# A selective-scan and attention block on one core: two PSUM banks for the jobs, new spacing, and the window softmax divided behind the values' product

## The reference, cut to what matters

```
h = exp(dt[:, :, None] * A) * h + (dt * xt)[:, :, None] * bt[:, None, :]     # the scan, for each t
y = einsum("bdn,bn->bd", h, ct)
scores = einsum(q of 32 tokens, k of the 96 tokens around) / sqrt(8) + bias, masked
attn   = softmax(scores, axis=-1)
ao     = attn @ v3 ;  attn_out = ao @ wo                     # 16 heads, 4 key/value heads
es     = x @ dec.T / sqrt(128) ; eo = softmax(es) @ dec      # memory lookup
x + 0.2*attn_out + 0.45*ssm_out + 0.15*silu(conv) + 0.2*(x @ w_wm + b + 0.3*eo)
```

## Time and profile before

| what | value |
|---|---|
| median of 3 runs | 1167.07 us (1165.49 to 1168.94) |
| the profiled execution | 1166.9 us, span 1165.1 us |
| busy DVE / POOL / PE / ACT | 988.3 / 951.5 / 866.0 / 835.1 us |
| granted TensorE clock, mean | 0.830 of full |

### The profile page before, as it was taken

One profiled execution on the slowest core, in us unless ns is written; L12 is line 12 of the kernel. 1 busy time (PEld: TensorE's weight loads), 2 busy tenths in 40 slices (PEclk: granted clock), 3 DMA queues, 4 the chain that ended last, 5 costly groups with the idle time before them and its releaser, 6 DMA issues. The chain is left out here.

```text
span 1165.1 us, 19124 instructions
## 1 busy us (share of the span) xinstructions
PE 866.0 (74%) x4151; PEld 361.1 (31%) x4151; DVE 988.3 (85%) x2306; ACT 835.1 (72%) x2247; POOL 951.5 (82%) x668
## 2 busy tenths in 40 slices
PE   4477769687786787777786777867768687778775
PEld 2132323232333233333232333323233233333332
DVE  2699998888897997979989799788998989898992
ACT  4668786877778776777777777587776876766671
POOL 6479997988888887888979898698887988788892
PEclk8558998778897977979889788787989788897797
DMA  5845766565756566566656476555666566656640
GB/s 121 202 127 147 199 164 171 133 169 163 181 153 159 156 158 165 146 155 167 165 166 165 118 192 169 141 147 148 173 167 177 137 166 169 174 157 173 159 113 9
DMA packets 124397, 181.18 MB, mean 156 GB/s; under 512 B 29266, under 2 KB 41062, under 8 KB 124262
## 3 DMA queue, kind: packets, MB, share of 16 engines
q1 hardware_dynamic: 123974, 179.56, 58.9%
q10 hardware_dynamic: 288, 0.20, 0.1%
HBM read 170.79 MB, written 5.05 MB: 151 GB/s over the span
## 5 line engine op out<-in xcount | busy, mean ns | idle before, releaser
L1391 POOL TENSOR_TENSOR prod<-hst,C 128x1024 f32<-128x1024 f32 x256 | 601.7, 2353 | 156.7 <-DVE hst L1201 155.9
L1201 DVE TENSOR_TENSOR_SCAN hst<-decay,bank 128x512 f32<-128x512 f32 x384 | 459.5, 1206 | 16.0 <-POOL prod L1391 15.1
L659 ACT ACTIVATE decay<-wide,A_rep 128x512 f32<-128x512 f32 x384 | 273.9, 715 | 72.8 <-DVE hst L1201 55.0
L1189 DVE TENSOR_TENSOR bank<-bank,B 128x512 f32<-128x512 f32 x384 | 261.7, 681 | 48.8 <-PE bank L938 23.0
L905 PE MATMUL bank<-spread,sel_bc 96*128 96x512 bf16 x384 | 170.0, 444 | 145.3 <-DVE hst L1201 137.0
L673 ACT ACTIVATE prob<-s_sb,nmax 128x96 f32<-128x96 f32 x512 | 184.8, 363 | 1.5 <-DVE nmax L1214 0.5
L1407 POOL TENSOR_TENSOR uwide<-uwide,B 128x512 f32<-128x512 f32 x128 | 162.7, 1271 | 21.8 <-DMA uwide<-u_rows 21.8
L929 PE MATMUL bank<-prod,sel_red 128*32 128x512 f32 x1024 | 171.7, 750 | 2.0 <-POOL prod L1391 2.0
L1201 DVE TENSOR_TENSOR_SCAN hst<-bank,uwide 128x512 f32<-128x512 f32 x128 | 155.0, 1211 | 6.1 <-ACT bank L659 4.6
L938 PE MATMUL bank<-k,q 128*128 128x384 f32 x256 | 133.6, 609 | 7.3 <-DVE nmax L1214 4.8
L945 PE MATMUL bank<-ident,prob 128*96 128x128 f32 x512 | 99.4, 328 | 48.9 <-ACT ao L689 44.2
(11 more groups left out here) (188 smaller groups left out, 1014.6 us busy)
## 6 DMA issues: line engine op xcount, KB each, us to landing
wide<-dt_rows SPq DMA_DIRECT2D x512, 256.0 KB, 4.6
uwide<-u_rows SPq DMA_DIRECT2D x128, 256.0 KB, 4.1
spread<-parts SPq DMA_DIRECT2D x66, 32.0 KB, 3.4
x_sb<-in_L_attn_x_dram SPq DMA_DIRECT2D x8, 256.0 KB, 4.1
dt_rows<-sp_t SPq DMA_DIRECT2D x8, 256.0 KB, 3.9
out_dram<-outb SPq DMA_DIRECT2D x8, 256.0 KB, 2.3
vw<-v_tok SPq DMA_DIRECT2D x80, 16.0 KB, 3.3
u_rows<-uv SPq DMA_DIRECT2D x8, 64.0 KB, 3.6
```

Of the source, the lines that this page charges most:

```text
L659: nc.scalar.activation(to, wide[m % SLOTS][:, s % 2, :], ACT.Exp, scale=A_rep[:, g:g + 1]).then_inc(exp_done, 1)
L1189: v.tensor_tensor(uP[s % 4][:, :], uP[s % 4][:, :], B2[p][:, :], ALU.mult).then_inc(dbx_done, 1)
L1201: v.tensor_tensor_scan(hst[:, s % 4, :], kept, into[:, :], 0.0, ALU.mult, ALU.add).then_inc(scan_done, 1)
L1391: g.tensor_tensor(prod[:, 2 * (m % 4):2 * (m % 4) + 2, :], hst[:, 2 * (m % 2):2 * (m % 2) + 2, :], C2[p][:, :].unsqueeze(1).to_broadcast([ ...
```

## The change

Four things change.

1. **Banks.** Bank 3 becomes `memP` and carries the nine "m" jobs; `jobP` keeps the others. `fill` keeps a predecessor for each of the two. The decay factors of q = 3 no longer lie in bank 3: the tile `decay` has four places in SBUF, and the scan of q = 3 reads `decay` and `uwide`.
2. **Spacing.** All jobs have new slots, the "m" jobs from slot 10 on (28 before), v, q and k of the next batch at 37, 52 and 56 (58, 60 and 62 before). Jobs are emptied one slot later than they are filled (`EMPTY_LAG` 1). Output comes three slots behind the feed-forward product (one before), the convolution's gate two slots behind its tanh (one before). In the last batch the ten first products of the projection stand in slots 48 to 63, where six stood in slots 58 to 63 and four behind the slots.
3. **Softmax.** The probabilities stay undivided. The transposition stands 6 slots behind the scores (9 before), the values' product 8 (11 before). Behind it PE multiplies the inverted sums, spread over 32 columns, by the identity, into columns 128 to 255 of the same bank; ACT copies both halves to `ao_raw`, and POOL multiplies them into `ao4` (`output_norm`, 9 slots behind the scores). `prob_norm` is gone.
4. **Value windows.** SP waits for the first scores of the batch, too, before it issues them.

```diff
-JOB_AT = {13: ("t", "back"), 15: ("p", "xaT"), 17: ("p", "xnT"), 19: ("p", "dtpre"),
-          22: ("t", "zT"), 26: ("t", "ffn"), 28: ("m", "es0"), 32: ("p", "B"), 33: ("p", "C"), 34: ("m", "pt0"),
...
+JOB_AT = {14: ("t", "back"), 18: ("p", "xaT"), 20: ("p", "xnT"), 22: ("p", "dtpre"), 24: ("t", "zT"),
+          28: ("t", "ffn"), 33: ("p", "B"), 35: ("p", "C"), 37: ("p", "v"), 52: ("p", "q"), 56: ("p", "k")}
+MEM_AT = {10: "es0", 15: "es1", 19: "pt0", 22: "es2", 27: "pt1", 31: "es3", 36: "pt2", 41: "conv", 47: "pt3"}
+EMPTY_LAG = 1
+LAST_PROJECT = {48: (0,), 50: (1,), 53: (2,), 54: (3,), 55: (4,), 56: (5,), 62: (6, 7), 63: (8, 9)}
...
-BIAS_LAG, EXP_LAG, INV_LAG, NORM_LAG, PT_LAG, PT_COPY_LAG, PV_LAG, AO_COPY_LAG = 2, (3, 4), 6, 5, 9, 9, 11, 11
+BIAS_LAG, EXP_LAG, INV_LAG, NORM_LAG, PT_LAG, PT_COPY_LAG, PV_LAG, AO_COPY_LAG = 2, (3, 4), 6, 9, 6, 6, 8, 8
...
-        uP, yP, sP, ptP, jobP = bank[0:4], bank[4], bank[5], bank[6], bank[7]
+        uP, memP, yP, sP, ptP, jobP = bank[0:POOL_Q], bank[3], bank[4], bank[5], bank[6], bank[7]
...
-        decay = sb("decay", [128, POOL_Q, L])
+        decay = sb("decay", [128, 4, L])
...
                 wait(sp, done["p"], job_count("p", B, "v"))
+                wait(sp, s_ready, B * NBLK + 1)
...
-                to = uP[q][:, :] if q == POOL_Q else decay[:, q, :]
-                nc.scalar.activation(to, wide[m % SLOTS][:, s % 2, :], ACT.Exp,
+                nc.scalar.activation(decay[:, q, :], wide[m % SLOTS][:, s % 2, :], ACT.Exp,
...
             def ao_copy(B, k):
                 wait(act, pv_ready, B * NBLK + k + 1)
-                if k == 0:
-                    wait(act, ready["t"], B * N_TAIL - N_TAIL + 1)
-                nc.scalar.activation(ao4[:, :, k * W:(k + 1) * W],
-                                     ptP[:, 0:128].rearrange("p (r q) -> p r q", r=REP), ACT.Copy).then_inc(ao_evac, 1)
+                wait(act, ao_norm, B * NBLK + k - 1)
+                nc.scalar.activation(ao_raw[:, k % 2, :, :].rearrange("p a c -> p (a c)"), ptP[:, 0:256],
+                                     ACT.Copy).then_inc(ao_evac, 1)
...
                 for g in range(KVH):
-                    ins = mm(ptP[32 * g:32 * g + HD, 0:128], vw[:, k, g, :], probT[:, g, :], start=True, stop=True)
+                    mm(ptP[32 * g:32 * g + HD, 0:128], vw[:, k, g, :], probT[:, g, :], start=True, stop=True)
+                wait(pe, p_inv, B * NBLK + k + 1)
+                for g in range(KVH):
+                    ins = mm(ptP[32 * g:32 * g + 32, 128:256], pinv[:, k % 4, g:g + 1].to_broadcast([128, 32]), ident[:, :],
+                             start=True, stop=True)
...
                 if q == POOL_Q:
                     wait(dve, gbx_done, B * GROUPS + i + 1)
-                    kept, into = uP[q][:, :], uwide[(i // 2) % U_SLOTS][:, i % 2, :]
+                    into = uwide[(i // 2) % U_SLOTS][:, i % 2, :]
...
-                v.tensor_tensor_scan(hst[:, s % 4, :], kept, into[:, :], 0.0, ALU.mult,
+                v.tensor_tensor_scan(hst[:, s % 4, :], decay[:, s % 4, :], into[:, :], 0.0, ALU.mult,
...
+            def output_norm(B, k):
+
+                wait(pool, ao_evac, B * NBLK + k + 1)
+                if k == 0:
+                    wait(pool, ready["t"], B * N_TAIL - N_TAIL + 1)
+                g.tensor_tensor(ao4[:, :, k * W:(k + 1) * W], ao_raw[:, k % 2, 0, :].rearrange("p (r q) -> p r q", r=REP),
+                                ao_raw[:, k % 2, 1, :].rearrange("p (r q) -> p r q", r=REP), ALU.mult).then_inc(ao_norm, 1)
```

More of the change, by code:

```diff
@@ L50 @@
-EMPTY_LAG = 0
-N_EARLY = 6
-JOB_SLOT = {name: s for s, (_, name) in JOB_AT.items()}
-AT = {
-    "reduce": 3, "y_copy": 5, "project": 1, "proj_copy": 12, "residual": 14, "aggr2": 16, "root2": 17,
-    "normalise2": 20, "ffn": 25, "output": 27,
-    "ln_stats": 0, "ln_aggr": 2, "ln_root": 4, "ln_apply": 11, "scale_xn": 12, "softplus_exp": 20,
-    "softplus_logs": 21, "rounding": 23, "log1p": 24, "dt": 25, "u": 27, "high": 30, "r": 32,
-    "mid": 35, "lo": 37,
-    "tanh": 39, "gate": 40,
+JOB_AT = {14: ("t", "back"), 18: ("p", "xaT"), 20: ("p", "xnT"), 22: ("p", "dtpre"), 24: ("t", "zT"),
+          28: ("t", "ffn"), 33: ("p", "B"), 35: ("p", "C"), 37: ("p", "v"), 52: ("p", "q"), 56: ("p", "k")}
@@ new lines @@
+MEM_AT = {10: "es0", 15: "es1", 19: "pt0", 22: "es2", 27: "pt1", 31: "es3", 36: "pt2", 41: "conv", 47: "pt3"}
+EMPTY_LAG = 1
+LAST_PROJECT = {48: (0,), 50: (1,), 53: (2,), 54: (3,), 55: (4,), 56: (5,), 62: (6, 7), 63: (8, 9)}
+MEM_SLOT = {name: s for s, name in MEM_AT.items()}
+AT = {
+    "reduce": 3, "y_copy": 5, "project": 1, "proj_copy": 13, "residual": 16, "aggr2": 18, "root2": 19,
+    "normalise2": 22, "ffn": 27, "output": 31,
+    "ln_stats": 0, "ln_aggr": 2, "ln_root": 4, "ln_apply": 13, "scale_xn": 15, "softplus_exp": 24,
+    "softplus_logs": 25, "rounding": 27, "log1p": 28, "dt": 29, "u": 30, "high": 32, "r": 34,
+    "mid": 36, "lo": 38,
+    "tanh": 42, "gate": 44,
@@ L86, in memory_tile_at @@
 def memory_tile_at(s, lag):
-    fam, name = JOB_AT.get(s - lag, ("", ""))
+    name = MEM_AT.get(s - lag, "")
     return int(name[2]) if name[:2] == "es" else None
@@ L778, in body @@
                         empty_job(*JOB_AT[s - EMPTY_LAG], B, p)
-                    fam, name = JOB_AT.get(s - 1, ("", ""))
+                    if s - EMPTY_LAG in MEM_AT:
+                        empty_job("m", MEM_AT[s - EMPTY_LAG], B, p)
+                    fam, name = JOB_AT.get(s - EMPTY_LAG - 1, ("", ""))
                     if fam == "p" and name in "qk" and not last(B):
@@ L854, in setup_step @@
                     pe.wait_ge(w_scaled, 4)
-            before = [None]
+            before = {"job": None, "mem": None}
             def fill(fam, B, name):
-                if before[0] is not None:
-                    f, b, n = before[0]
+                held = before["mem" if fam == "m" else "job"]
+                if held is not None:
+                    f, b, n = held
                     wait(pe, done[f], job_count(f, b, n))
@@ L865, in filled @@
                 ins.then_inc(ready[fam], 1)
-                before[0] = (fam, B, name)
+                before["mem" if fam == "m" else "job"] = (fam, B, name)
             def pre_job(name, B, p, front=False):
@@ L941, in prob_transposes @@
             def prob_transposes(B, k):
-                wait(pe, p_norm, B * NBLK + k + 1)
+                wait(pe, p_exp, B * NBLK + k + 1)
                 wait(pe, ao_evac, B * NBLK + k)
@@ L965, in mem_job @@
             def mem_job(name, B, p):
+                if name == "es0":
+                    wait(pe, done["m"], B * N_MEM)
                 fill("m", B, name)
@@ L968, in mem_job @@
                     t = int(name[2])
[L969 removed]
+                    ins = mm(memP[:, :], xaT[p][:, HALO + t * 128:HALO + (t + 1) * 128], decTs[:, :], start=True,
                              stop=True)
@@ L992, in project @@
                 elif n < 10:
-                    wait(pe, ao_evac, (B + 1) * NBLK)
+                    wait(pe, ao_norm, (B + 1) * NBLK)
                     ins = mm(jobP[:, :], wo_p[:, n - 6, :], ao4[:, n - 6, :], start=False, stop=False)
@@ L1026, in body @@
             def body(B, p):
-                before[0] = ("p", B, "v")
+                before["job"], before["mem"] = ("p", B, "k"), None
                 for s in range(UNITS):
@@ L1060, in body @@
                         pre_job(name, B + 1, 1 - p)
-                    if fam == "m" and name != "conv":
-                        mem_job(name, B, p)
-                    if last(B) and 0 < s - JOB_SLOT["pt3"] <= N_EARLY:
-                        project(B, p, s - JOB_SLOT["pt3"] - 1)
+                    if s in MEM_AT and MEM_AT[s] != "conv":
+                        mem_job(MEM_AT[s], B, p)
+                    if last(B):
+                        for n in LAST_PROJECT.get(s, ()):
+                            project(B, p, n)
             def tail(B, p):
-                for n in range(N_EARLY, N_PROJ - 1):
-                    project(B, p, n)
                 reduce_group(B, GROUPS - 1)
@@ L1220, in inverse_sums @@
                 wait(dve, p_exp, B * NBLK + k + 1)
-                wait(dve, p_norm, B * NBLK + k - 3)
+                wait(dve, pv_ready, B * NBLK + k - 3)
                 v.reciprocal(pinv[:, k % 4, :], psum_r[:, k % 4, :]).then_inc(p_inv, 1)
```

42 lines of the change are left out of this document (19 added, 23 removed), and 2 rows, old and new, of the table JOB_AT.

## The result

The changed kernel takes 1201.24 us (median of 4 runs, 1199.22 to 1206.44) beside 1167.24 us of the kernel before: ratio 1.030, interval 1.026 to 1.033. It is slower by 34 us. The forecast was 1212 us, slower. Where a kernel had an execution far off its others (1267.38 us at a granted clock of 0.625 among ten in experiment 5, 3778.41 us among four in experiment 7), the median given counts it and the ratio leaves it out.

The account below looks back on a forecast made before the run. No engine is full; DVE has least room, so its waits and instruction lengths set the end. From 1166.9 us: -86.4 removed waits, +38.5 slot 8, +3 small items, +89.6 scans = 1211.6, forecast 1212; range 1120 to 1260.

Parts of the forecast that it names:

- The scan with two SBUF inputs: DVE's 128 scans of q = 3 each wait 0.70 us for the running POOL instruction: 89.6 us more.
- Who is made longer on POOL: POOL is held up to 1.21 us by each scan; its 2.35 us products get a second group about 1.2 longer.
- The wait in slot 8: PE waits for value windows, so DVE waits 5.5 us for unit 12's u in 7 batches: 38.5 us more.
- Waits taken away: DVE's waits for output, scores, u, gate, ACT, POOL's product and at the end shrink by 86.4 us in sum.
- the port: Mutual exclusion of a DVE scan with two SBUF inputs and a POOL instruction; forecast price 0.70 us a scan.
- The product of the sums: Four more matmuls a block on PE, 0.42 us a block, at no cost by itself; POOL's normalisation drops to 450 ns.
- The sum: Profiled 1166.9 us, less 86.4, plus 38.5, 3 and 89.6, gives 1211.6 us; forecast 1212.
- the 3 us for SP's front and slot 27: First batch's windows waiting for first scores, plus bunched feed-forward, memory and reduction matmuls in slot 27: 3 us more.
- The free port: Rival, chance 0.15: a scan with two SBUF inputs doesn't exclude POOL; 1122 us, faster.
- The gap: Rival, chance 0.17: scans meet POOL as it changes instruction and pay 0.3 us each; 1160 us.
- the worst alignment: Rival, chance 0.18: each scan comes just behind the input product's start and waits 1.1 us; 1263 us.

Follow-up runs that it names:

- experiment 5: Kernel before with only the new softmax order, old PE lags, POOL's product 12 slots behind the scores: 1171.60 us, ratio 1.003 to the kernel before.
- experiment 7: Kernel before with an adapted spacing only: one bank for jobs, q = 3 decay in PSUM, old softmax: 1155.27 us, ratio 0.990 to the kernel before.
- Experiment 1: Kernel before with one edit, the decay factors of q = 3 moved from bank 3 to SBUF: 1209.45 us, ratio 1.038 to the kernel before.
- experiment 2: Changed kernel whose q = 3 scans read bank 2 in PSUM instead of `uwide` (not the reference's output): 1133.91 us, ratio 0.975 to the kernel before.
- Experiment 3: Changed kernel with the 12 value window DMAs issued earlier, in three portions of four: 1174.35 us, ratio 1.007 to the kernel before.

## Why the prediction was right, step by step

- **The scan with two SBUF inputs: right in kind, the term was too large.** Forecast 0.70 us for each of 128 scans, 89.6 us; measured 1751 - 1211 = 540 ns, 69.1 us. Experiment 1 makes it appear with that edit alone, experiment 2 makes it vanish. The Trainium skill's rule (SBUF — State Buffer, "Who interferes with whom"), of which the prediction said that no run showed it for a scan, is thereby shown for one: whole instruction by whole instruction. Of the 128 scans 83 began inside a product (0.59 us longer on average), 30 inside an input product (0.68), and 15 met nothing; on the timeline of before it was 89, 23 and 8 with the rest on short ones. A few more met the input product, as foreseen, but with a mean rest of 0.83 us there and not 0.99. Over all 128 the mean rest was 0.65 us, what I had laid out; the 0.05 that I added for a POOL that catches up did not come. The rest of the error is that I let a held scan take its full 1.21 us behind the wait. It takes 1.08, so its price is the rest less 0.13 us, and a rest of under 0.13 costs nothing. Summed over the 128 scans that gives 540 ns a scan, as measured. With it 28 of 128 paid nothing.
- **Who is made longer on POOL: wrong.** I expected a second group of products 1.2 us longer. All 256 products keep 2353 ns. The input product behind them got longer, from 1.27 us without a meeting to 1.87, 77 us in all, and so did the few other instructions that stood there (eight normalisations and six steps of the softplus). The reason lies in the order of the work. What stands behind the product of a pair is the input product; and the next large product needs the very scan that is waiting, so it can't have begun and be held up by it. Up to 1.21 us a scan was my bound for POOL; 77/128 = 0.60 was paid.
- **The wait in slot 8: right, the place in the order one off.** Forecast 5.5 us seven times, 38.5 us; measured 5.96, 41.7. PE's wait was 5.44 in batch 4, where I had 5.3, and the clock 0.50 as taken. But DVE did not meet it at the u of unit 12. It met it one slot earlier, at `scores_there` of block 3, with the values' product, the sums and one product of the projection ahead of these scores; the transposes and the u that I had counted stand behind them. In batch 4 DVE asked 1.2 us before PE went on and then waited 5.0 us for matmuls, where I had it ask 0.2 us behind PE, with up to 6.8 us of them. The two differences nearly cancel, so that the agreement in size is in part luck. Experiment 3 removes the wait; only 27 of the 42 us are then gained.
- **Waits taken away.** Output 28.3 forecast and 28.3 measured; u 7.3 and 7.1; ACT 4.9 and 4.9; the gate 12.9 and 15.3. The end also gained its 2.0 us, which the list shows at `x` (8.9 to 6.9): the last reduction now stands right behind POOL's last product. Two were too large. Of the 23.0 us for scores 19.6 stood at a batch's start and all but 0.2 of them went, but 12.0 us of waits for scores inside the batch, in slots 25 and 41 mostly, stand under the same name, where 3.5 did before. And of the 8 us for POOL's product only 2.2 went; with the port taken out (experiment 2) 11.9 of the 15.1 go, so that POOL had lost its room again to the port. With 1.4 more at the softplus and some 6 us in small rows, 75.4 us went, for 86.4.
- **The product of the sums: right.** 56.3 us for 128 blocks, 0.44 us each, for 0.42; the normalisation took 454 ns at the median for 450, and 523 on average, since twelve were held, eight of them behind a scan. Not foreseen: the first `output_norm` of a batch waits for the projection of the batch before, 29.9 us in 7 times on POOL. In experiment 3 that wait is gone, too, so it is a consequence of PE's standing, and no cost of its own.
- **The sum.** Forecast -86.4 + 38.5 + 3 + 89.6 = 44.7 us over the profiled execution before; measured 32.3. In the same terms that is -75.4 + 41.7 + 66.0, the last one all of DVE's growth. The port's term was 20 us too large, and the removed waits 11 us too large, with opposite signs, so that the sum, 12 us off, is nearer than the port's term by luck. No row shows the 3 us for SP's front and slot 27, and SP's new wait for the first scores was not tested by itself.
- **The rivals.** The free port falls with experiments 1 and 2, and its time, 1122, is close to what experiment 2 measured with the port truly free, 1134. The gap (0.3 us) and the worst alignment (1.1 us) fall with 0.54. The measured price lies above the 0.35 us from which the change is slower.

## What to carry to other kernels

Before an operand moves from PSUM to SBUF to make room for something else, count which DVE instructions then have both inputs in SBUF and how busy GpSimd is beside them: here 128 scans of 512 turned a gain of 2.5% into a loss of 3%, and seven such instructions in the old trace were enough to foresee the sign. When lags are shortened, follow each operand of the instruction that comes earlier back to its DMA, and its place in the issuing queue. And a change that bundles four things is best taken apart: with one bank and the decay left in PSUM the spacing made the kernel 1.0% faster, the softmax alone made it no faster, and the two together 3.3%.
